# Mixer kernel on Trainium2: two small turnings moved from the middle of a slot to its end, one product moved a slot later

## The reference, cut to what matters

```python
proj = xn @ in_proj_w.T             # gate, hbc, dt
xBC  = silu(causal_conv4(hbc))      # x, B, C of 8 groups, 64 heads
dt_p = softplus(dt + dt_bias)
dA   = exp(dt_p * -exp(A_log))      # a decay per token and head
state = state * dA + dt_p * x * B   # scan over tokens;  y = state . C
y = rmsnorm_per_group(y + x * D) * norm_weight * silu(gate)
s = y @ out_proj_w.T
# four-stream block
x_pre = sum_n softmax(xn_rms @ W_pre.T)[n] * streams[n]     # 256 channels
branch = x_pre @ W_branch
f = sinkhorn(res_logits) @ streams + branch * h_post[n]
```

## Time and profile before

| | |
|---|---|
| Runs | 3021.14 us median of 3 (3020.88 to 3022.29) |
| Profiled execution | 3022.99 us, span 3021.5 us |
| PE busy | 2972.3 us (98%) |
| DVE busy | 2138.0 us (71%) |
| ACT busy | 1717.2 us (57%) |
| POOL busy | 834.1 us (28%) |
| HBM traffic | 147 GB/s over the span |
| Projection, L1125 to L1127 | 7728 matmuls, 389 to 395 ns each |
| Output, L1414 to L1416 | 3072 matmuls, 389 to 404 ns each |

### The profile page before, as it was taken

The page is one execution under the profiler, slowest core; times in us unless marked ns, Lnnn a source line. Parts: engine busy times, 40 slices in busy tenths (PEclk is TensorE's granted clock), DMA queues, the critical chain, the costliest instruction groups (busy, mean ns, idle before and its releaser), DMA issues.

```text
span 3021.5 us, 44616 instructions
## 1 busy us (share of the span) xinstructions
PE 2972.3 (98%) x14160; PEld 2320.8 (77%) x14160; DVE 2138.0 (71%) x2678; ACT 1717.2 (57%) x3744; POOL 834.1 (28%) x561
## 2 busy tenths in 40 slices
PE   8999999999999998999999999999999999999998
PEld 7777777777777776777777777777776888888876
DVE  7676667676766676767667676767677878678767
ACT  5666575657566675475665757575665232244443
POOL 3222332333323355323233223323233100001112
PEclk9999999999999999999999999999999999999999
DMA  3425342524334353534342434343353544466655
GB/s 130 156 105 181 106 160 91 181 99 152 139 111 174 122 192 100 162 119 140 112 175 92 158 111 174 101 150 138 129 190 107 178 145 145 146 209 213 223 198 179
DMA packets 126872, 444.99 MB, mean 147 GB/s; under 512 B 21360, under 2 KB 25584, under 8 KB 110352
## 3 DMA queue, kind: packets, MB, share of 16 engines
q1 hardware_dynamic: 118352, 421.17, 40.5%
q0 software_dynamic: 4640, 16.78, 1.5%
q10 hardware_dynamic: 3744, 5.51, 0.6%
HBM read 397.92 MB, written 45.48 MB: 147 GB/s over the span
## 4 chain that ended last, share of the span: by engine, by line
PE 75%; issue 6%; DMA 5%; POOL 4%; DVE 4%; ACT 3%; SPq 1%; ACTq 0%; DVEq 0%; POOLq 0%
PE bank L1125 16%; PE bank L1127 15%; PE bank L1126 15%; PE bank L1170 8%; PE bank L1414 6%; PE bank L1415 6%; PE bank L1416 6%; POOL gate L506 2%; PE bank L1138 2%; DMA acc<-in_w_out 2%; PE bank L1156 1%; DMA y_scratch<-gate 1%; DMA units<-cum_scratch 1%; POOL nrstd L494 1%; DVE acc L862 1%
## 5 line engine op out<-in xcount | busy, mean ns | idle before, releaser
L1125 PE MATMUL bank<-x_hi,w_hi 128*128 128x512 f32 x2576 | 1017.3, 395 | 8.4 <-DVE acc L862 4.8
L1127 PE MATMUL bank<-x_hi,w_lo 128*128 128x512 f32 x2576 | 1001.3, 389 | 0.0
L1126 PE MATMUL bank<-x_lo,w_hi 128*128 128x512 f32 x2576 | 1001.0, 389 | 0.0
L1125 PEld LDWEIGHTS bank<-x_hi,w_hi 128*128 128x128 f32 x2576 | 484.4, 188 | 122.4 <-issue 19.5
L1127 PEld LDWEIGHTS bank<-x_hi,w_lo 128*128 128x128 f32 x2576 | 484.3, 188 | 101.9
L1126 PEld LDWEIGHTS bank<-x_lo,w_hi 128*128 128x128 f32 x2576 | 484.8, 188 | 95.2
L862 DVE SCALAR_TENSOR_TENSOR acc<-bank,conv_w,acc 128x511 f32<-128x511 f32 (+2 forms) x576 | 429.8, 747 | 179.6 <-ACT acc L635 150.5
L844 DVE TENSOR_TENSOR w_lo<-w_raw,w_hi 128x1024 fp32r<-128x1024 f32 x160 | 227.8, 1424 | 357.9 <-ACT w_hi L619 357.7
L488 POOL TENSOR_TENSOR sums<-sums,sq 128x512 f32<-128x512 f32 x96 | 191.1, 1991 | 911.4 <-ACT sq L695 911.4
L903 DVE TENSOR_TENSOR units<-units,bc 128x2560 f32<-128x2560 f32 x128 | 387.1, 3025 | 54.3 <-ACT units L682 54.3
L672 ACT ACTIVATE units<-units,falls 128x128 f32<-128x128 f32 x1024 | 325.9, 393 | 149.7 <-DMA units<-cum_scratch 149.7
(11 more groups left out here) (169 smaller groups left out, 3253.3 us busy)
## 6 DMA issues: line engine op xcount, KB each, us to landing
units<-cum_scratch SPq DMA_DIRECT2D x128, 1280.0 KB, 8.2
w_raw<-in_w_in SPq DMA_DIRECT2D x160, 512.0 KB, 3.7
xbc<-y_scratch SPq DMA_DIRECT2D x126, 512.0 KB, 3.6
acc<-in_w_out SPq DMA_DIRECT2D x126, 256.0 KB, 3.8
y_scratch<-gate SPq DMA_DIRECT2D x30, 1024.0 KB, 5.3
xbc<-in_x SPq DMA_DIRECT2D x16, 512.0 KB, 5.5
units<-in_x SPq DMA_DIRECT2D x16, 512.0 KB, 3.7
rstd_b<-rc_scratch SPq DMA_DIRECT2D x16, 512.0 KB, 4.2
```

Of the source, the lines that this page charges most:

```text
L1125: pe.matmul(out, w_hi[m % 2][:, k, :], hi, start=(k == 0), stop=False)
L1126: pe.matmul(out, w_hi[m % 2][:, k, :], lo, start=False, stop=False)
L1127: mm = pe.matmul(out, w_lo[m % 2][:, k, :], hi, start=False, stop=(k == KT - 1))
```

## The change

It touches plan FIRST alone. PE projects the whole slot first. Behind it come `turn_cum` (now in slots 6 and 7), `turn_mixed` (still slots 4 to 11), and then `early`, in which the branch product of tile t now stands in slot t+5 (slots 5 to 12). On ACT the copy of the turned branch moves to slot t+5 and that of the product to slot t+6. ACT's copies of the turned sums stay in slots 7 and 8. SP, POOL and DVE have the same programs as before.

```diff
-EARLY_TURN, CUM_TURN = 4, 7
+EARLY_TURN, CUM_TURN = 4, 6
...
-            t = s - EARLY_TURN - 1
+            t = s - EARLY_TURN - 2
             if 0 <= t < NT:
                 act.wait_ge(e.branch_done, t + 1)
...
-            t = s - EARLY_TURN
+            t = s - EARLY_TURN - 1
             if 0 <= t < NT:
                 act.wait_ge(e.mix_turned, t + 1)
...
-            t = s - EARLY_TURN
+            t = s - EARLY_TURN - 1
             if 0 <= t < NT:
                 if t == 0:
                     pe.wait_ge(e.branch_w_loaded, 16)
...
                 elif s > 1:
-                    project(g, s, (0, KT // 2))
+                    project(g, s)
+                if plan is FIRST:
+
                     if 0 <= s - CUM_TURN < SEQS:
                         turn_cum(half, s - CUM_TURN)
                     if 0 <= s - EARLY_TURN < NT:
                         turn_mixed(half, s - EARLY_TURN)
-                    project(g, s, (KT // 2, KT))
-                if plan is FIRST:
                     early(half, s)
```

## The result

The kernel after took 3031.3 us, the median of 12 executions, against 3021.2 us for 12 of the kernel before. One of the 12 executions of the kernel after took 11804.6 us and is left out of the ratio, which is 1.0028, with a 95% interval of 1.0020 to 1.0035: **slower by 8.5 us**, 6.0 to 10.6 (the medians differ by 10.1). The forecast was 3026.0, within 0.2%, with a range to 3028.8. The measured time lies above that range. The same kernel, run again in two of the three series of the experiments, each on another chip, gave 1.0049 (1.0035 to 1.0063) and 1.0039 (1.0025 to 1.0053).

The account below looks back on a forecast made before the run. PE, busy for 98% of the span, was taken as the bound. Half 0 (4.2 + 1.7 - 1.16 = +4.7) and half 1 (1.3 - 1.16 = +0.1) gave +4.9 us on the median 3021.14: 3026.0, range 3023.6 to 3028.8.

Parts of the forecast that it names:

- PE bound, and the moved wait: PE is busy 98% of the span; its slot 8 wait goes, a wait for the tables comes at slot 6's end.
- Half 0: End of slot 6: PE waits 77.52 to 81.69, 4.2 us, then slow clock costs 1.7; with savings +4.7 us.
- The savings, -1.16 us in each half: Slots 4 to 12: turnings -0.64, slot 8's wait -0.70, the product's restart in slot 12 +0.18 us.
- the 0.08: Saving in us for each turning moved from mid-slot to the slot's end, eight times in each half, 0.64 us.
- Half 1: End of slot 6: PE arrives at 1229.29, tables at 1230.57, wait 1.3 us; with savings +0.1 us.
- half 0's wait should bring the low level and half 1's should not: Behind the table waits: PE's clock falls to 1.2 GHz after 4.2 us idle, costing 1.7 us, not after 1.3.
- The sum: Both halves' changed stretches together: +4.7 and +0.1, in all +4.9 us before rounding, 0.16%.
- Rival 1 of the prediction: End of slot 6, half 0: clock low longer after the wait, 4.35 us lost, +7.5 in all, 3028.7; chance 0.27.
- the rival's 4.35: Microseconds lost to slow clock, half of the 8.7 us slow stretch read at the kernel's start, behind its first transposes.
- The rest at nothing: Later POOL mix 5, stream and weight loads, sums' copies and stores: priced at nothing, covered by PE's three to four slots.

Follow-up runs that it names:

- wait in half 0 alone: The kernel after with the far tables made in slot 5 in half 1 only, still slot 6 in half 0: 3027.8 us, ratio 1.0017 against before.
- filled kernel: The kernel after with 13 unneeded matmuls ahead of the sums' turning in slot 6, run twice: ratios 1.0016 and 1.0017 against before.
- sums late: The kernel after with the sums turned at the ends of slots 7 and 8, run twice: ratios 0.9995 and 0.9995 against before.
- only the sums early: The kernel before with only the sums' turning moved, to the ends of slots 6 and 7: 3030.8 us, ratio 1.0015 against before.
- tables in slot 5: The kernel after with DVE making the far tables in slot 5 instead of 6, ahead of the split of weight tile 4: 3025.2 us, ratio 1.0000.

## Why the prediction was wrong, point by point

- **PE bound, and the moved wait.** Right. The new wait is at L1285, nothing later in the kernel gave it back as far as scatter lets it be seen, and the waits at L1272 went.
- **Half 0.** Right to a tenth in the first trace: arrival 77.5, tables at 81.56 (81.69 forecast), wait 4.1 (4.2), slow stretch 3.4 us (3.3), stretch +4.75 (+4.7). For the slow clock that was luck in part: behind the same wait the second trace has 4.8 us, which costs 0.7 us more, and the kernel with the wait in half 0 alone has 5.1.
- **The savings, -1.16 us in each half.** Right in sum in half 0: -1.2 in the four traces of the versions without a wait there. In half 1 the four without a wait there give -1.1 to -1.2, with the slow clock of slot 4 taken off. The terms are not all right. The turning and the product start 0.22 us apart and not 0.14, but the slots are 6.58 us apart (92.06 to 98.64) where they were 6.64 (71.94 to 78.58), so 0.06 of the 0.08 is there, 0.48 of the 0.64 us. Which of the other terms makes up the difference no run shows.
- **Half 1: this step failed.** It is PE's arrival, "1230.35 - 1.06 = 1229.29", with the wait of 1.3 us that comes of it, and with it "half 0's wait should bring the low level and half 1's should not". The wait was 3.1, 2.7 and 4.3 us in three traces, and 3.0 with half 0's wait taken away, and a slow stretch followed it each time. The arrival was taken from one trace, in which the clock was low for some 6 us behind slot 4's wait. The earlier trace rows show 5.7 of them; this window of the kernel before has the rise in it, at about 1212.8:

```profile
1212.00:1213.00 1.00, 1.00 (x5) 0.58 0.90 369
```

  In the three traces of the kernel after it was low there for 3.4, 3.1 and 0 us. Half of what is missing to 6.1 brings PE earlier by 1.35, 1.5 and 3.05 us, and the tables, timed from slot 4's start by DMA, ACT and DVE, came 0.5, 0.0 and 0.1 us later than reckoned (23.86). With the 1.3 that makes 3.15, 2.8 and 4.4 us; 3.07, 2.72 and 4.26 were measured. So what PE gains at the first wait it loses at the second, and behind the second, now of 2.7 us or more, the clock fell once more. Against the mean of the two traces before, half 1 cost 2.6, 1.9 and 3.0 us instead of 0.1. The tables were forecast well: 23.86 us held within half a microsecond.
- **The sum.** 4.9 for the two stretches, 7.3 to 7.9 measured: 2.4 to 3.0 short, most of it in half 1 (1.7 to 2.9), the rest in half 0 (0.9 in the second trace). The 8.5 (6.0 to 10.6) of the result covers that. The 14.8 and 11.8 of the second and third series of the experiments lie above; their traces, both of the fastest execution of their series, don't show the remainder. Only a small part is the clock: averaged over 21 executions of the kernel after the granted clock was 0.9943, over 87 of before 0.9956, so 0.0013 x 3030 = 3.9 us lost, against the 3.4 of two shortest slow stretches; within each of these two series the same working gives 4.4 and 5.0 us. Where the rest of those two series went stays open.
- **Rival 1 of the prediction** (the clock low for longer, since transposes follow the wait). It had the right sign, and 8.5 us is near its 7.5, but that is chance: the slow stretch behind the wait in half 0 was 3.4, 4.8 and 3.4 us in the three traces of the kernel after, under the 5.6 from which this rival was to decide, and the kernel before shows 3.3 and 6.1 behind ordinary matmuls. The Trainium skill (TensorE: Matmul & The Clock Gate, Part 4: PE-mode transpose) says that the full rate does not engage for transposes; the runs don't bear that out: the ten transposes took 1.09 us with the clock up and 1.87 us with it down (81.61 to 83.48), and in the filled kernel the clock stayed at the full level behind them. The start, on which the rival's 4.35 rested, is slow by the spacings alone; the granted clock in the windows of the kernel before doesn't show it:

```profile
16.00:17.00 1.00, 1.00 (x7) 1.00 1.03 422
```

- **The rest at nothing.** Right: POOL's mix 5 began at 92.62, as said, and SP's load of streams behind it at 97.06, 5.1 us later than before; no new wait of PE in slots 7 to 13. (By the code `load_bx(t)` waits for mix t-2, its buffer's last reader, not t-1; the forecast's times follow the code.)

## What to carry to other kernels

When a step is moved earlier on the engine that bounds the kernel, time its input from the engine that makes it and ask what that is timed from. If it hangs on another chain, every microsecond that PE gains ahead of it turns into waiting, so the forecast needs the earliest arrival, not that of one trace. And give an idle time of about 3 us a price of its own for what follows it. Two changes took the loss away: the sums turned a slot later, and the three small instructions of the tables put ahead of a weight split that stood before them only by the order of the program. Neither beats the kernel before by anything that can be told (0.9995 and 1.0000).

## What the runs showed of the hardware

An idle time of PE of 2.7 to 3.4 us may or may not bring the clock down, in one and the same place. At slot 4 of half 1, 3.33 us did in the kernel before; 3.30 in sums late and in the third trace of the kernel after, and 3.36 in only the sums early, did not. At the tables 2.72, 3.00 and 3.07 us did, 3.18 with only the sums early did not. All six waits of 4.1 us and more at the tables did, and so did 4.00 us (in two traces) and 5.89 us at slot 4 of half 1. The slow stretches behind the waits for the tables were 3.1 to 5.4 us long, so that a wait of 4 us costs PE about 6 to 7 us.

Shorter idle times are not safe either. In the kernel with the tables in slot 5 the clock fell behind 1.82 us, far from the change, in PE's timeline and windows:

```profile
280.36 0.47 PE L1125 MATMUL bank<-x_hi,w_hi 128*128 128x512 f32 x1 [1.82 <-ACT gate L660]
```

```profile
281.20:284.50 3.30, 3.30 (x9) 0.50 0.00 0
```

It also fell behind 1.83 us in sums late (1566.93) and behind 2.25 us in only the sums early (2881.26), and not behind 1.94 us in the kernel with the wait in half 0 alone (1577.50). The 1.4 us at slot 4 of half 0 never brought it down, in 14 traces.
